# Last attention loop of a four-layer network: two of every eight products with the edge counts go from VectorE to GpSimd (POOL), with a semaphore for each place of the ring

## The reference, cut to what matters

```python
h = (x_flat @ W_gat).reshape(M, HEADS, NUM_EXPERTS)          # HEADS = NUM_EXPERTS = 4
a_src = (h * att_src).sum(-1)
a_dst = (h * att_dst).sum(-1)
e = jax.nn.leaky_relu(a_src[src] + a_dst[dst], negative_slope=0.2)
e_max = jax.ops.segment_max(e, dst, num_segments=M)
ee = jnp.exp(e - e_max[dst])
denom = jax.ops.segment_sum(ee, dst, num_segments=M)
alpha = ee / (denom[dst] + 1e-16)
msg = h[src] * alpha[:, :, None]
agg = jax.ops.segment_sum(msg, dst, num_segments=M)
```

## Time and profile before

| | |
|---|---|
| median of three runs | 844.78 us (843.91 to 844.96) |
| the profiled execution's own time | 843.78 us |
| its span, first to last instruction | 842.0 us |
| busy: PE, DVE, ACT, POOL | 613.4, 553.4, 388.4, 249.9 us |
| the loop's first weigh starts at | 731.1 us |
| its last weigh starts at | 810.2 us |

### The profile page before, as it was taken

How to read it: one execution, slowest core, us unless ns; L and a number is a source line. 1 busy time by engine, 2 the same in 40 slices (tenths; PEclk the granted TensorE clock), 3 DMA queues, 4 the chain that set the end, 5 groups by cost and what they waited for, 6 DMA issues and landing times. The chain is left out here.

```text
span 842.0 us, 8346 instructions
## 1 busy us (share of the span) xinstructions
PE 613.4 (73%) x2468; PEld 363.7 (43%) x2468; DVE 553.4 (66%) x1322; ACT 388.4 (46%) x587; POOL 249.9 (30%) x193
## 2 busy tenths in 40 slices
PE   4543879999974995639977658995789742987860
PEld 2442657777753742524444324353355310641110
DVE  2894576777755535659456648536876697769966
ACT  2002658787844602525365414702336420559930
POOL 4995357788853002010066405001100000000000
PEclk9999999999985996768965567965979855579995
DMA  3440000000003104020000020002000000000000
GB/s 102 126 121 4 1 1 1 2 0 1 2 0 88 16 1 141 1 72 7 1 0 1 1 58 20 1 1 59 14 6 2 14 0 0 1 0 0 0 0 13
DMA packets 18453, 18.47 MB, mean 22 GB/s; under 512 B 10946, under 2 KB 14339, under 8 KB 18024
## 3 DMA queue, kind: packets, MB, share of 16 engines
q1 hardware_dynamic: 18408, 17.94, 8.1%
HBM read 17.04 MB, written 0.26 MB: 21 GB/s over the span
## 5 line engine op out<-in xcount | busy, mean ns | idle before, releaser
L647 POOL TENSOR_TENSOR l0f_hid_lo<-l0f_hid,l0f_hid_hi 114x512 fp32r<-114x512 f32 (+1 forms) x75 | 97.9, 1314 | 55.2 <-ACT l0f_hid_hi L729 54.3
L825 DVE TENSOR_TENSOR l0f_hid<-l0f_silu,PS 114x512 f32<-114x512 f32 x96 | 65.7, 686 | 40.7 <-ACT l0f_silu L746 39.6
L683 PE MATMUL PS<-l0f_xs,l0w_hi 128*114 128x512 f32 x192 | 78.3, 408 | 0.0
L683 PE MATMUL PS<-l0f_xs,l0w_lo 128*114 128x512 f32 x192 | 77.1, 401 | 0.0
L746 ACT ACTIVATE l0f_silu<-PS 114x512 f32<-114x512 f32 x96 | 57.6, 601 | 30.9 <-PE PS L683 30.1
L2417 PE MATMUL PS<-l3f_ring,l3f_slots 128*32 128x512 f32 x128 | 55.5, 659 | 13.0 <-DVE l3f_ring L2496 13.0
L729 ACT CAST l0f_hid_hi<-l0f_hid 114x512 fp32r<-114x512 f32 x96 | 59.1, 615 | 2.7 <-DVE l0f_hid L825 2.2
L1303 POOL TENSOR_TENSOR l2c_den<-l2c_far,l2c_den 128x1024 f32<-128x1024 f32 x16 | 37.5, 2357 | 64.7 <-ACT l2c_den L1461 64.7
L2441 ACT ACTIVATE l3f_ring<-l3r_plain,l3r_neg 128x1024 f32<-128x1024 f32 x32 | 36.0, 1134 | 22.9 <-PE PS L2397 13.2
L2496 DVE SCALAR_TENSOR_TENSOR l3f_ring<-l3f_ring,l_countT 128x1024 f32<-128x1024 f32 x32 | 38.7, 1216 | 9.9 <-ACT l3f_ring L2445 9.9
L2490 DVE SCALAR_TENSOR_TENSOR l3f_ring<-l3f_slope,l3r_low,l3f_ring 128x1024 f32<-128x1024 f32 x32 | 40.7, 1276 | 1.0 <-ACT l3f_ring L2441 1.0
(11 more groups left out here) (548 smaller groups left out, 1404.9 us busy)
## 6 DMA issues: line engine op xcount, KB each, us to landing
l0w_raw<-in_l_w SPq DMA_DIRECT2D x32, 170.5 KB, 3.2
l3k_edge<-in_edges SPq DMA_DIRECT2D x2, 1024.0 KB
l2c_wqkv<-in_l_wqkv SPq DMA_DIRECT2D x3, 384.0 KB, 4.2
l0w_w<-in_l_w SPq DMA_DIRECT2D x8, 142.5 KB
l2f_raw<-in_l_w SPq DMA_DIRECT2D x2, 512.0 KB, 6.0
l1c_pos_w<-in_l_pos_w SPq DMA_DIRECT2D x1, 784.0 KB, 4.9
l1c_vrow<-l1c_vimg SPq DMA_DIRECT2D x7, 88.0 KB, 3.7
l1f_raw<-in_l_w SPq DMA_DIRECT2D x2, 256.0 KB
```

The lines of the kernel that those rows point to most:

```text
L647: g.tensor_tensor(hid_lo[0:k, q % HIDS, :], hid[0:k, q % HIDS, :], hid_hi[0:k, q % HIDS, :], ALU.subtract).then_inc(S("low_pool"), 1)
L683: last = t.matmul(m.PS[0:k, (one, two)[z], :], half[:, e, z, a:a + k], xs[:, h * HALF:(h + 1) * HALF], start=(half is ew.hi), stop=(half i ...
L825: v.tensor_tensor(hid[0:k, at % HIDS, :], silu[0:k, at % RING0, :], m.PS[0:k, two, :], ALU.mult).then_inc(S("free"), 1)
```

## The change

`BY_POOL = (2, 6)` names the places u whose product with the counts goes to POOL: 2 of 8, in four passes 8 products of 32. POOL waits for the exp of the step as DVE did. Its product is a plain `tensor_tensor` multiplication, without the min with 1. As the products are then finished by two engines and not in order, the one semaphore `weighed` becomes eight, one for each place, and PE waits for that of the place, with the number of the pass.

```diff
+BY_POOL = (2, 6)
...
-                t.wait_ge(S("weighed"), RING3 * i + (u + 1))
+                t.wait_ge(S(f"weighed{u}"), i + 1)
...
+    @block.gpsimd
+    def _(g):
+        with g.Fori(0, NB // 2) as i:
+            for u in BY_POOL:
+                g.wait_ge(S("exp"), RING3 * i + (u + 1))
+                g.tensor_tensor(out=buffer(u), in0=buffer(u), in1=counts_of(i, u), op=ALU.mult).then_inc(S(f"weighed{u}"), 1)
...
-            v.scalar_tensor_tensor(out=buffer(u), in0=buffer(u), scalar=1.0, in1=counts_of(i, u), op0=ALU.min, op1=ALU.mult).then_inc(S("weighed"), 1)
+            v.scalar_tensor_tensor(out=buffer(u), in0=buffer(u), scalar=1.0, in1=counts_of(i, u), op0=ALU.min, op1=ALU.mult).then_inc(S(f"weighed{u}"), 1)
...
-            weigh(i, u)
+            if u not in BY_POOL:
+                weigh(i, u)
```

## The result

The changed kernel takes 849.57 us (median of four, 849.18 to 851.44), the kernel before 844.35 us on the same chip (four, 843.71 to 844.96). The ratio is 1.0066, 95% interval 1.0049 to 1.0084: 0.66% slower, where 0.9% slower was forecast.

What follows compares the result with a forecast made beforehand. DVE was taken to bound the loop; seven POOL products at +1.04 us each (2.17 held up, 1.13 spared) add 7.3 us to the median, giving 852 us (+0.9%), range 848 to 858.

Steps and rivals of the forecast that it cites:

- The mechanism: In the loop: DVE sets the pace; each POOL product shuts DVE out for its length, sparing one weigh of 1.13 us.
- The price of a product: Per POOL product of 2.36 us: DVE held up 2.17 us, less a spared weigh of 1.13, net +1.04 us.
- Which smaller or weigh is held up: POOL's step 22 product enters when smaller of step 23 ends; weigh of step 21 then ends 2.17 us later.
- Seven of eight: Seven of the eight POOL products lie on DVE's path, +7.3 us together; the first costs nothing.
- the stop: First pass: DVE idles 7.73 us before its weigh at 750.75; what it is spared ahead of that counts nothing.
- The sum: Whole kernel: +1.04 us for each of seven products, +7.3 us, forecast 852 us or +0.9%.
- PE and ACT don't take over: Loop pass: DVE's new 21.0 us stays above ACT's 17.13 and PE's 15.22.
- that rival: After a held-up weigh PE's clock falls to half; +1.9 us after the last weigh, 854 us in all; chance 0.06.
- No exclusion: Smaller and weigh run untouched beside POOL, ACT becomes the bound; about -6 us, 839 us; chance 0.11.
- DVE keeps the port: Waiting POOL is not let in until DVE stops with the ring empty; +10 us, 855 us; chance 0.13.
- Semaphores: Around POOL's products: the added waits are PE's, and POOL's on exp; no time was charged for them.

Runs made afterwards that it cites:

- e2: Changed kernel, but smaller and weigh each read one operand from PS instead of SBUF (other values computed): 836.99 us, ratio 0.9944, loop 77.66 us.
- e3: Kernel before, with one operand each of smaller and weigh read from PS instead of SBUF: 843.15 us, ratio 1.0004, loop 81.95 us.
- e6: Changed kernel, but POOL writes a constant to an unused table instead of each product, reading nothing: 837.74 us, ratio 0.9938, loop 76.06 us.
- e5: Kernel before, DVE keeping all 32 weighs, plus eight POOL products into an unused table that nobody waits for: 856.17 us, ratio 1.0173.
- e4: Changed kernel run again unaltered, for a second profile: 850.18 us, ratio 1.0086 against the kernel before, loop 88.59 us.
- e8: Changed kernel, but smaller takes a constant 0.0 instead of its scalar from SBUF: 852.16 us, ratio 1.0122, loop 91.41 us.
- e1: Kernel before with only the semaphore split into eight; all 32 products stay with DVE: 842.93 us, ratio 1.0002, loop 82.13 us.
- f3: Changed kernel, Relu of steps 3 and 7 in PS, POOL's full product waiting for the weigh two steps before: 846.35 us, ratio 1.0041.
- e7: Changed kernel, but weigh reads its constant 1.0 from a column in SBUF: 851.15 us, ratio 1.0113, loop 89.76 us.

## Why the prediction was right, point by point

- **The mechanism.** Right: DVE sets the pace, each POOL product shuts it out for nearly its whole length, and one weigh is spared. e2 and e3 show the condition on DVE's side (two SBUF tensors, for smaller and weigh; the slot copy is held up with one), e6 the other side of it (POOL reads), e5 the price alone.
- **The price of a product.** Forecast +1.04, measured +0.97 (+0.96 to +1.01). POOL's 2.36 us were right: where it waited for nothing it took 2.347 to 2.368. The hold-up is 2.10, not 2.17, and the 0.07 us lie in the overlaps. At its beginning POOL overlaps DVE by 0.15 us (2.36 - 2.21) and at its end by 0.18 (the smaller ends at 787.86, 1.09 after POOL, and takes 1.27 alone), 0.33 together. I took 0.13 for each, 0.26.
- **Which smaller or weigh is held up.** Wrong place, same price. I had POOL let in at the next end, behind the smaller of step 23, and weigh of step 21 held up. It came in one instruction later, and the next smaller paid; so its products took 4.09 us in the middle, and not a little over 3. The price does not depend on who pays, and so this error did not touch the sum. Since the exp is ready 3.5 us early, a product that ends a turn later still ends in time: PE's step behind it waits 0.30 us.
- **Seven of eight.** Right: the one ahead of the stop costs 0.01 us. But the product of step 6 cost +0.64 (1.61 less 0.97), not the full price. It fell on the slot copy at 754.35 (2.37 us for 0.21). In the kernel before, the weigh at 758.25 waited 0.28 us for an exp that ACT's table load had made late; after the change DVE is late itself, and that wait is gone. The prediction had the full price for it.
- **The sum.** Forecast +7.3; 7 x 0.97 = 6.79, less 0.33 for step 6 and with 0.01 for the first product, gives 6.47 as measured. The pass was forecast at 21.0 us and is 20.84. The whole time was forecast at 852 and is 849.57. The medians differ by 5.2 us here and by 7.0 in e4 (850.18 against 843.15), on either side of the loop's 6.47; what lies ahead of the loop scatters by more than that.
- **PE and ACT don't take over.** Right: 13.90 and 14.35 us of 19.00. From 751 us to the closing matmul PE's clock is 1.00 in both kernels, so that rival did not happen; ahead of that, in the first pass, it is 0.50 in both.
- **The rivals.** "No exclusion" is refuted for this pair of instructions and came true, with its size, as soon as POOL read nothing (e6). "DVE keeps the port" I held at 0.13 against rows of another DVE line; in e8 it came true for two pairs of products of four. What changed between the two kernels was a thing that I had not looked at, that smaller takes its scalar from SBUF. So it is luck in part that the rival did not come true in the change itself: nothing in the prediction said that smaller would let POOL in.
- **Semaphores.** They were costed at nothing without a reason; e1 bears that out.

## What to carry to other kernels

An idle POOL is not free help for a busy DVE. Before an elementwise product of two SBUF tensors is moved there, look at what DVE runs beside it: if its instructions read two SBUF tensors, the move costs POOL's duration less a quarter of a microsecond and wins only DVE's pitch for one (here 2.10 against 1.13, for 128 x 1024 float32), and it is free only where DVE waits anyway, as with the first product here. The loop gets shorter once one of DVE's tensors lies in PS or POOL only writes (e2, e6), though a copy from SBUF to SBUF in DVE's list still waits for a POOL that reads (e2); but the part of POOL's work that reaches past such a DVE instruction is paid in full (f3), so count the overlap from POOL's real start.

## What the runs showed of the hardware that I had not expected

- Who lets POOL in: with DVE's instructions back to back, a waiting POOL product got through at the latest ahead of the next product or minimum of two SBUF tensors that fetches its scalar from SBUF. In mid-loop it took 3.07 or 3.08 us where both of DVE's do (e7) and 4.09 where every second does (the change). Where none does (e8), two of eight waited for 11 and 12 us, with two more piled up behind them, and four got through after one instruction (2.4 to 2.9 us). At slot copies and at instructions with a constant it got through some times and others not; the rule behind that is open.
- A long record is not always a hold-up. Beside a POOL product that reads, the slot copy took 2.37 us and the next smaller started 2.30 us after it (the change, 754.35 and 756.65); beside POOL's memset the copy's record grew to 0.88 to 2.10 us, and yet the next instruction started 0.13 or 0.14 us after it (e6). Read the distance from start to start, not the duration.
- A loop of this kind repeats within hundredths of a microsecond from one execution to another (88.59 and 88.59; 82.12, 82.13 and 82.10 for kernels that differ in nothing that counts), while the stages ahead of it scatter by several. One trace with two marks told more here than a median of whole times.
